# A graph layer on one core: the tables of steps are worked out in small pieces between the rounds of the edge stage

## What is computed

```python
h = relu(layernorm(x))                       # per node, 256 features
msg = relu(h[src] + edge_attr)               # per edge
p = msg @ W_fc.T + b_fc                      # 256 wide
scores = p @ Q.T                             # 4 heads
alpha = segment_softmax(scores, dst)         # over the edges of one node
pooled[h] = segment_sum(alpha[:, h] * p, dst)
gate = softmax(segment_mean(p, dst) @ Wg.T + bg)
out = x + sigmoid(sum_h gate[:, h] * pooled[h])
```

## Time and profile before

| what | value |
|---|---|
| median of 3 runs | 752.02 us (751.45 to 756.54) |
| the profiled execution | 750.41 us, of it the span from the first to the last instruction 748.6 us |
| mean granted clock of TensorE | 0.92 of full speed |
| busy share PE, DVE, ACT, POOL | 73%, 67%, 51%, 59% |

### The profile page before, as it was taken

One profiled execution on the slowest core, in us unless ns is written; L12 is line 12 of the kernel. 1 busy time (PEld: TensorE's weight loads), 2 busy tenths in 40 slices (PEclk: granted clock), 3 DMA queues, 4 the chain that ended last, 5 costly groups with the idle time before them and its releaser, 6 DMA issues.

```text
span 748.6 us, 12544 instructions
## 1 busy us (share of the span) xinstructions
PE 545.8 (73%) x2436; PEld 419.2 (56%) x2437; DVE 504.4 (67%) x1835; ACT 378.9 (51%) x649; POOL 443.1 (59%) x335
## 2 busy tenths in 40 slices
PE   2323888888788988788400988998878788778784
PEld 1212666666666665567300777776666566556563
DVE  2057777877778987788899766666656555554552
ACT  0004555655556665557202145566666666666673
POOL 5771666666663366650000155777878887787797
PEclk9755999999999999999855899999999999999998
DMA  4531555555554478875300499989999999999998
GB/s 137 161 99 35 170 170 172 167 168 166 166 169 141 127 225 258 279 222 205 113 0 0 139 298 391 377 278 346 328 350 331 339 336 330 328 337 314 340 347 300
DMA packets 135483, 171.42 MB, mean 229 GB/s; under 512 B 8533, under 2 KB 122027, under 8 KB 135445
## 3 DMA queue, kind: packets, MB, share of 16 engines
q10 hardware_dynamic: 90496, 89.83, 36.4%
q1 hardware_dynamic: 32101, 42.99, 18.5%
q0 software_dynamic: 12848, 38.20, 15.8%
HBM read 111.39 MB, written 59.59 MB: 228 GB/s over the span
## 4 chain that ended last, share of the span: by engine, by line
PE 48%; DVE 14%; ACT 9%; issue 9%; another core or an unknown queue 8%; ACTq 3%; POOL 3%; DVEq 2%; DMA 2%; SPq 1%; POOLq 0%
PE bank L621 21%; PE bank L687 19%; PE bank L611 6%; ACT arena L497 4%; DVE spread L1006 3%; ACT bank L473 2%; POOL arena L383 2%; ACTq L500 1%; DVEq L1010 1%; ACT arena L430 1%; DMA out_dram<-arena 1%; ACTq L452 1%; DVEq L1006 1%; DVE stats L804 1%
## 5 line engine op out<-in xcount | busy, mean ns | idle before, releaser
L687 PE MATMUL bank<-p_keep,spread 128*128 x1172 | 273.4, 387 | 51.8 <-DVE spread L1006 40.7
L383 POOL TENSOR_TENSOR arena<-arena 128x1024 f32<-128x1024 f32 x96 | 224.8, 2351 | 142.0 <-ACT arena L497 141.0
L1006 DVE TENSOR_SCALAR spread<-bank,rel,wgt 128x128 f32<-128x128 f32 x586 | 195.7, 404 | 128.4 <-PE bank L687 84.8
L687 PEld LDWEIGHTS bank<-p_keep,spread 128*128 128x128 f32 x1172 | 218.2, 191 | 107.9 <-issue 80.7
L621 PE MATMUL bank<-w_all,arena 128*128 128x264 f32 (+1 forms) x784 | 220.9, 406 | 43.6 <-ACT arena L430 25.9
L621 PEld LDWEIGHTS bank<-w_all,arena 128*128 128x128 f32 (+1 forms) x784 | 139.4, 198 | 68.6 <-ACT arena L430 31.5
L370 POOL DMA_INDIRECT p_keep<-in_x_dram,idx x124 | 122.8, 990 | 83.5 <-PE bank L621 44.5
L497 ACT ACTIVATE arena<-bank 128x1024 f32<-128x1024 f32 x97 | 99.2, 1023 | 142.7 <-PE bank L687 124.6
L430 ACT ACTIVATE arena<-bank 128x256 f32<-128x256 f32 x196 | 73.5, 375 | 104.6 <-PE bank L611 54.4
L370 POOL DMA_INDIRECT arena<-in_x_dram,idx x72 | 70.1, 974 | 57.6 <-ACT arena L422 24.5
L473 ACT ACTIVATE bank<-zero 128x1024 f32<-128x1024 f32 x98 | 100.5, 1026 | 3.0
(11 more groups left out here) (188 smaller groups left out, 177.6 us busy)
## 6 DMA issues: line engine op xcount, KB each, us to landing
out_dram<-arena ACTq DMA_DIRECT2D x97, 512.0 KB, 4.5
arena<-in_x_dram ACTq DMA_DIRECT2D x73, 512.0 KB, 5.4
arena<-in_edge_attr_dram SPq DMA_DIRECT2D x48, 512.0 KB
arena<-in_x_dram POOLq DMA_DIRECT2D x24, 512.0 KB, 5.9
p_spill<-p_keep SPq DMA_DIRECT2D x16, 512.0 KB
p_keep<-p_spill SPq DMA_DIRECT2D x16, 512.0 KB, 5.7
p_keep<-in_x_dram,idx POOLq DMA_INDIRECT x124
arena<-in_x_dram,idx POOLq DMA_INDIRECT x72
```

Source lines behind the costliest of these rows:

```text
L383: pool.tensor_tensor(yout[:, slot, :, :], yout[:, slot, :, :], xin[:, slot, :, :], ALU.add).then_inc(summed, 1)
L687: nc.tensor.matmul(places[:, bass.ds(place, T)], spread[:, k0 + k, :], p_rows[:, bass.ds(p_at, T)], start=False, stop=True, skip_group_che ...
L1006: v.tensor_scalar(spread[:, k, :], bank[:, 7, P:2 * P], rel[:, bass.ds(s0 + k, 1)], wgt[:, bass.ds(s0 + k, 1)], ALU.is_equal, ALU.mult).th ...
```

## The change

The tables are no longer made ahead of the edge stage. `table_work(k)` puts 41 pieces, one to a round, behind DVE's round k for k from 4 to 16 and from 24 to 51; each raises `table_step`, and a later one waits for the count that it needs. PE's sums over tiles stand behind its rounds 20 (`sum_small`, 19 products with one column), 32 to 44 (`sum_rel`, four times two of 147 columns) and 48 and 52 (`sum_tiles`, two of 294 columns each), all in bank 7; ACT copies their results out in rounds 34 to 54. The tables of the path now stand with one half round (6 steps) or one group of three to a partition, in `tab` and `tab_i`; as words they go to HBM and come back into one row (`words`, SP, ahead of edge load 18 and 21). `rel` is summed from differences of neighbouring tiles (`change`, with `dst` loaded once more one tile further, `later_i`) and is not reduced by the node, and the column numbers in bank 7 are shifted by the first destination instead. The scratch takes 16 slots of `p_keep` instead of 34.

The start is changed as well: the indices of the first eight tiles come by a transfer of their own that turns them on its way, POOL's memsets of `src_i`, `dst_i` and `next_i` go to DVE, the weights are issued on ACT's queue, `tables_ready` is gone, and `b_rep` is read as a broadcast. Line numbers below 250 differ little, those of the engines' programs by up to 165.

```diff
-            sp.wait_ge(pads_set, 3)
...
+            with nc.allow_non_contiguous_dma(reason="the indices of the first tiles, turned, once"):
+                sp.dma_start(idx[:, 0:FIRST], src[0:FIRST * P].rearrange("(t e) -> e t", e=P)).then_inc(first_in, 16)
+            sp.wait_ge(pads_set, 1)
+            load_tiles(src_i, src, 0, src_in)
+            load_ea(0)
+            load_ea(1)
+            sp.wait_ge(pads_set, 2)
+            load_tiles(dst_i, dst, 0, dst_in)
+            load_ea(2)
+            sp.wait_ge(pads_set, 3)
+            load_tiles(later_i, dst, P, later_in)
+            load_ea(3)
...
+            for quad in range(4, QUADS):
+                if quad == 18:
+                    sp.wait_ge(table_step, 40)
+                    sp.dma_start(words_out, words).then_inc(words_stored, 16)
+                if quad == 21:
+                    sp.wait_ge(words_stored, 16)
...
-            sp.wait_ge(tables_ready, 1)
+            sp.wait_ge(words_in, 64)
...
-            pool.wait_ge(idx_ready, 1)
+            pool.wait_ge(first_in, 16)
...
-                if t == RING - 34:
-                    pool.wait_ge(tables_ready, 1)
+                if t == FIRST:
+                    pool.wait_ge(idx_ready, 1)
+                if t == RING - TAIL:
+                    pool.wait_ge(table_summed, PARTS + 3)
...
+            act.dma_start(w_nat, w_fc.rearrange("(c p) d -> p c d", p=P)).then_inc(w_in, 16)
...
+            def copy_rows(to, n):
+                act.wait_ge(table_summed, n + 2)
+                nc.scalar.activation(to, bank[:, 7, 0:to.shape[1]], ACT.Copy).then_inc(rows_copied, 1)
...
-            pe.wait_ge(before_ready, 1)
-            for b in range(BLK):
-                nc.tensor.matmul(bank[:, 2, 0:P], ones[:, :], ended[:, b, :], start=(b == 0), stop=(b == BLK - 1))
-            for b in range(BLK):
-                nc.tensor.matmul(bank[:, 3, b * P:(b + 1) * P], ones[:, :], diag[:, b, :], start=True, stop=True)
-            by_step(lambda b: ones[:, :], before, 0, lo_summed)
-            pe.wait_ge(sel_ready, 1)
-            by_step(lambda b: dst_f[:, b, :], sel_0, 4, rel_summed)
-            pe.wait_ge(tables_ready, 1)
+            def sum_small():
+                pe.wait_ge(table_step, 13)
+                for j in range(HALF):
+                    for b in range(BLK):
+                        n = rows_in_block[b]
+                        nc.tensor.matmul(bank[0:HALVES, 7, j:j + 1], after[0:n, b, j:COLS:HALF], ones[0:n, 0:1],
+                                         start=(b == 0), stop=(b == BLK - 1))
...
+            def sum_rel(part):
+                if part:
+                    pe.wait_ge(rows_copied, part)
+                else:
+                    pe.wait_ge(table_step, 16)
...
+            pe.wait_ge(idx_ready, 1)
             for k in range(TILES + MUL_LAG):
                 if 0 <= k - TURN_LAG < TILES:
                     turn(k - TURN_LAG)
+                if k == MUL_LAG:
+                    pe.wait_ge(w_ready, 1)
                 if 0 <= k - MUL_LAG:
                     multiply(k - MUL_LAG)
+                if k == 20:
+                    sum_small()
+                elif k == 32:
+                    sum_rel(0)
...
+                elif k in (10, 11):
+                    dve.wait_ge(table_step, 6)
+                    v.tensor_scalar(after[:, k - 10, :], count_i, step_of[:, k - 10:k - 9], None, ALU.is_gt
+                                    ).then_inc(table_step, 1)
...
+                elif k == 24:
+                    dve.wait_ge(table_summed, 1)
+                    v.tensor_copy(tile_nj, bank[0:HALVES, 7, 0:HALF]).then_inc(table_step, 1)
...
+                if k == -2:
+                    finish_weights()
+                table_work(k)
...
+            v.tensor_scalar(bank[:, 7, P:2 * P], column[:, :], dst_0, None, ALU.subtract)
```

More of the change, by code:

```diff
@@ new lines, in _ @@
+            load_ea(3)
+            sp.wait_ge(pads_set, 4)
+            with nc.allow_non_contiguous_dma(reason="one node for each tile, twice, once"):
+                ends_of = dst[0:whole].rearrange("(t e) -> t e", e=P)
+                sp.dma_start(next_i[1:P, 0, 0:1], ends_of[0:P - 1, P - 1:P]).then_inc(next_in, 16)
+                sp.dma_start(next_i[0:TILES - P, 1, 0:1], ends_of[P - 1:TILES - 1, P - 1:P]).then_inc(next_in, 16)
+                sp.dma_start(next_i[0:P, 0, 1:2], ends_of[1:P + 1, 0:1]).then_inc(next_in, 16)
+                sp.dma_start(next_i[0:TILES - 2 - P, 1, 1:2], ends_of[P + 1:TILES - 1, 0:1]).then_inc(next_in, 16)
+                sp.dma_start(next_i[TILES - 2 - P:TILES - 1 - P, 1, 1:2],
+                             dst[whole:whole + 1].rearrange("(t e) -> t e", e=1)).then_inc(next_in, 16)
@@ L585, in _ @@
             last.then_inc(wq_done, 1)
[L587 to L589 removed]
+            rows_in_block = (P, COUNT_ROW)
+            def sum_small():
+                pe.wait_ge(table_step, 13)
+                for j in range(HALF):
                     for b in range(BLK):
[L591 to L593 removed]
@@ new lines, in sum_small @@
+                nc.tensor.matmul(bank[:, 7, HALF + 3:HALF + 4], dst_f[:, 0, :], ident[:, 0:1],
+                                 start=True, stop=True).then_inc(table_summed, 1)
+            def sum_rel(part):
[3 more added lines that the diff above has]
+                    pe.wait_ge(table_step, 16)
+                for b in range(BLK):
+                    n = (P, COUNT_ROW + 1)[b]
+                    last = nc.tensor.matmul(bank[:, 7, 0:PART], change[0:n, b, :],
+                                            after[0:n, b, part * PART:(part + 1) * PART],
+                                            start=(b == 0), stop=(b == BLK - 1))
+                last.then_inc(table_summed, 1)
@@ L605, in turn, with sum_tiles @@
+            def sum_tiles(half):
+                pe.wait_ge(rows_copied, PARTS + half)
+                for b in range(BLK):
+                    n = rows_in_block[b]
+                    last = nc.tensor.matmul(bank[:, 7, 0:2 * PART], ones[0:n, :],
+                                            after[0:n, b, half * 2 * PART:(half + 1) * 2 * PART],
+                                            start=(b == 0), stop=(b == BLK - 1))
+                last.then_inc(table_summed, 1)
             def turn(t):
@@ L690, in _ @@
             pe.wait_ge(wgt_ready, 1)
+            pe.wait_ge(words_in, 64)
             pe.sem_inc(stepped, AHEAD)
```

358 lines of the change are left out of this document (226 added, 132 removed).

## The result

The changed kernel takes **741.84 us** (median of 4 runs, 738.11 to 745.5) against 751.74 for the kernel before (4 runs): ratio 0.9879, 95% interval 0.9839 to 0.9919, 1.2% faster. Forecast were 732, 2.7%. Its profiled execution took 745.5, the slowest of the four, with a span of 743.8.

What follows compares the result with a forecast made beforehand. Start and tables, much of it waiting for late results, then PE and DVE in the edge stage bound the kernel. 750.4 - 45.6 + 3 + 11 + 9.8 + 1.5 + 0.3 = 730.4; median 732 us, range 704 to 748.

Steps and rivals of the forecast that it cites:

- The head start: Start of the edge stage: without tables ahead, product 0 comes at 24.1 us instead of 69.7, saving 45.6 us.
- The rule on small pieces: Start: a strided last dimension takes one descriptor per element, so the turned index load might make the sum 6 us worse.
- DVE's pieces: Edge stage, tiles 4 to 51: 41 table pieces, 8.8 us of work, mostly in idle time; 3 us on the path.
- PE's sums: Edge stage: the tables' sums on PE, 13.4 us of work, mostly on the path; 11 us (0 to 14).
- 0.1 us a tile to spare: Edge stage without late results: PE's most idle time, 1.18 - 1.06 us a tile, so its table sums mostly lengthen the path.
- rival 3: Edge stage: long waits belong to the tables' seven groups of sums themselves; 50 us more, 782 us; chance 0.07.
- The gathers under the stage: Edge stage: 25 gathers formerly issued ahead of it now run during it, at 0.39 us each; 9.8 us.
- 9.8 + 1.5: Edge stage: 9.8 us for 25 gathers moved under it, 1.5 us for the first 19 tiles losing their slightly faster pace.
- rival 2: Start's late results move into the stage: PE held 20 of 28 us from 24 to 52, replacing 9.8; 742 us; chance 0.20.
- The prediction's closing doubt: Whole forecast: wrong if late results follow something the rows don't show, such as how far POOL is ahead; no size given.
- the 0.3: Weights part: one more DVE instruction stands ahead of it, costing 0.3 us.
- The second rule of the Trainium skill: Edge stage: DVE's two-port operations lock GpSimd out of writing descriptors; six wide pieces would delay gathers by 2.6 us, 735 us.

Runs made afterwards that it cites:

- b_late: The kernel before with its first gather put off until the tables are ready; 779.9 us (one run).
- a_paced: The changed kernel, POOL still up to 36 gathers ahead, with a 512-column POOL fill that POOL waits for between gathers 12 to 35; 738.46 us (one run).

## Why the prediction was wrong in its size

**The head start: right.** Forecast 45.6 us; measured 46.7, with gather 0 at 4.79 (forecast 6.0) and product 0 at 22.99 (24.1). The rule on small pieces, which the prediction took from the Trainium skill (DMA: Bandwidth & Descriptors, "Rules for kernel authors"), is not contradicted as to their number, but the turned load of 4 KB landed 3.5 us after its issue, and nothing of the 6 us appeared.

**DVE's pieces, 3 us: about right.** 3.7 with the first landings on the free chip, not visible on the holding one.

**PE's sums, 11 us: too high by a few us.** The first group cost 4.2 us on the holding chip and 5.3 on the free one (forecast 7). The six others were forecast at most of 6.4 and cost nothing to 2.1. The working's "0.1 us a tile to spare" sets only L621's 1.06 us against 1.18 and leaves out the turn; and where it has DVE set the pace without holds, its own row has PE as full, 15.00 of 15 us. No long hold stood behind L666, L682 or L691, and b_late shows L591 answered at once: rival 3 is out.

**The gathers under the stage, 9.8 us: the step that failed.** The prediction priced a gather that moves into the stage by the mean of the steady stage, 0.39 us. There POOL is bound to PE: if PE is held, POOL stops too, and the hold ends. The gathers that moved were the first 36, which POOL issues without waiting for anybody, and such a run held PE, DVE and ACT for as long as it went on, and some 9 us longer. In place of 9.8 + 1.5, tiles 0 to 10 cost 31.5 us more than before (product 0 to eviction 10: 47.5 us against 16.0). On the free chip the same stretch costs 3.7 us more (18.7 against 15.0), so some 28 us are the hold. Then POOL was its 36 ahead, and no more was lost. That is the mechanism of **rival 2**, given 0.20, and its sign came true: PE was busy for 11.34 of the 35 us from 25 to 60. That its 742 also meets the 741.84 is in part luck. Its hold was 20 us, not 28, its sum kept 11 us for PE's sums, which cost 4, and of the 13.2 us that the changed kernel is ahead when the walk begins, only 9.9 are in the medians. The argument used against it, that no wait in the stage was above 4 us, came from a stretch in which POOL paused; the earlier trace rows had the case without pauses in them, 20 us late, at the same 1.27 us a gather. The prediction's closing doubt, how far POOL is ahead, was the right one.

**The sum.** 46.7 - 31.5 - 1.7 (between tiles 10 and 195) is 13.5 at the stage's end; forecast were 20.3 there. The weights part took 53.9 us against 53.6, the 0.3 as forecast.

**The second rule of the Trainium skill** (SBUF — State Buffer, "Who interferes with whom"): the gathers beside the two wide compares (L864), at 61.69 and 63.16, took 1.17 and 1.19 us, where the median is 0.95. So the trace does agree with a delay, of 0.2 us each and some 0.5 us in all, where the prediction reckoned 2.6 by the rule. The gather of 1.22 us at 76.15 before, by which the prediction set the rule aside, was no case without a wide piece beside it: it starts 0.01 us behind DVE's `add_edge` (L810, 0.41 us, two inputs). In the changed kernel 18 of 196 gathers take over 1.05 us. One is the first, two stand beside L864, and the 15 others all start within 0.15 us of the start of an `add_edge` (L969); of the gathers that start 0.15 to 0.6 us behind one, none does.

**Open:** by what path a run of gathers delays word from PE and DVE, why hardly ACT's, and why only on some chips. Every run on record carries a recorded span and clock, so whether the recording takes part in the holds is open as well. A smaller gather was not tried on the chip, so whether rows, bytes or the number of gathers count is open too. Nor was the lead of 20 seen on a free chip.

## What to carry to other kernels

A price read from a steady stretch holds only where what limits it is the same; before moving work, ask whether the engine that hurts the others will have to wait for them in the new place. A producer that may run ahead needs a bound for its start, too: here a lead of 24 beat the kernel before by 2.1 to 2.8% on both kinds of chip, and 20 by 4.1% on a holding one, where the change itself, with 36, gave 1.2 to 2.1%. The best number for one chip (16) was 1.5% slower than before on the other, so settle such a bound on more than one.

## What the runs showed of the hardware

- Gathers of 128 rows issued by POOL each 1.25 us without a pause delay word of PE's and DVE's instructions on a holding chip: it came up to 20 us late before, and engines waited for it for up to 13 us in the changed kernel and 16 in b_late. For ACT's word nobody waited over 1.6 us in the changed kernel. With 1.76 us from gather to gather nothing was held for long. From an idle start, it took 16 to 21 us of such a run before it showed (held from 24.9 with the first gather at 8.78 before; from 25.7 with it at 4.79 after; from about 60 with it at 39.29 in b_late); in a_paced, where gathers had gone on with pauses, some 7 us (run from 61.0, word late from about 68).
- A gather that POOL starts within 0.15 us of the start of DVE's `add_edge`, which reads two tiles, takes 1.1 to 1.2 us in most cases in place of 0.95, on both kinds of chip.
- The same kernel took 751 to 757 us on two chips and 677 to 678 on another, though a gather's time on POOL (946 ns median) and the weights part (53.6 us) were equal on both.
- Plain loads of the same 128 KB on the same queue took POOL 0.54 us and held nobody.
